# Shorter arithmetic on VectorE in a two-layer graph and mixture-of-experts network: reciprocal roots in 8 linked operations for 11, experts' ranks in 3 operations for 6

## The chip, the cores and the metric

The kernel is one program on one core of a Trainium2 chip, started once. The metric is the device time of that program in microseconds (us); a median of several executions without a profile is given, and one further execution was taken with the hardware profiler. The engines are TensorE (PE, and PEld for its weight loads), VectorE (DVE), ScalarE (ACT), GpSimd (POOL) and the queue that issues most transfers (SP). Each engine runs its own instructions in program order and waits on semaphores for the others.

## The reference

The input is a batch of 128 graphs ("tiles") of 128 nodes with 128 features, and a dense 128x128 adjacency for each. Four steps follow each other, each of the form x = x + f(...):

```python
x = x + L0_gnn(layernorm(x), adj)        # adj @ x, @ W1 (512 wide), rms norm, silu, @ W2
x = x + L0_ffn(layernorm(x), edges)      # attention over 524288 edges gives 4 scores a node; 2 of 4 experts
x = x + L1_gnn(layernorm(x), adj)        # masked softmax attention within a tile, elu
x = x + L1_ffn(layernorm(x))             # softmax over 8 gates, 2 of 8 experts
```

Every `layernorm` and the rms norm need 1/sqrt of a variance for each node. The layer norm inside the expert choice of `L0_ffn` needs it too. Both expert layers pick the two largest of 4 (or 8) values for each node, a tie going to the lower index. The experts are computed for all nodes, and the gates of those not chosen are zero.

## The kernel before

Nodes lie on the 128 partitions. Four tiles make a group (`TB = 4`), so there are 32 groups. The program has four stages one behind the other: `sort_and_gin` (tiles named front_ and sort_), which sorts the edges on VectorE while it computes the first graph layer and the first layer's expert outputs, group by group; `find_blocks` and `edge_tables` (find_, att_), which build tables; and `layers` (lay_), which does the rest. There is no planner: the order on each engine is that in which the code is written out by hand.

In `sort_and_gin`, VectorE runs for each group `sort(g, 0)`, two `hidden` (L705), `sort(g, 1)`, two `hidden`, `sort(g, 2)`, the rms root (L742, then `rsqrt`), a copy and an addition, `sort(g, 3)`, `sort(g, 4)`, then the addition of the second product (L757), which waits for TensorE, and `norms` (L716 to L723 with `rsqrt` in between). `scale` on ScalarE waits for the rms root, and the next group's TensorE work for the normalised rows.

In `layers`, each round `i` of a loop handles four blocks of edges (`attend`), the first layer's four experts of group `m = i - 2`, the attention of group `t = i - 3`, and the second layer's eight experts of group `f = i - 4`. VectorE's order in a round is:

```python
attend(b); expert(0, m, 0); elu(t); expert(0, m, 1); choose(f); expert(0, m, 2)
attend(b + 1); expert(0, m, 3); bias(0, m); end_elu(t); norms(t); expert(1, f, 0); expert(1, f, 1)
attend(b + 2); expert(1, f, 2); shift(t); expert(1, f, 3); [scores]; expert(1, f, 4)
attend(b + 3); expert(1, f, 5); weigh(m); expert(1, f, 6); expert(1, f, 7); bias(1, f); [two_best]
```

`scores` and `two_best` run in every second round only, for eight tiles at once. `choose` and `scores` call `rank`; `norms` and `scores` call `rsqrt`. `expert` is line L2174; for the second layer it waits for TensorE's product (L1800) and signals `y_added`, on which TensorE's product for the expert two further on waits. `attend` ends in the split of the messages (L1066 to L1069); TensorE's segment sum (L1777) waits for it. `shift` (L2256) waits for TensorE's gate logits (L1890).

`me.link(...)` issues an operation that raises a semaphore and lets VectorE wait for that semaphore before its next operation. `me.mark(...)` raises it without the wait, and `me.wait()` waits for all marked.

Of the kernel before, what the change touches and what calls it, by code (L numbers as in the profile page):

```python
# [9 lines left out]
I32 = mybir.dt.int32  # L10
U16 = mybir.dt.uint16
BF16 = mybir.dt.bfloat16
ALU = mybir.AluOpType
# [3 lines left out]
P = 128  # L17
LN_EPS = 1e-05
RMS_EPS = 1e-06
NEG = -9000000000000000.0  # L20
SLOPE = 0.2
TB = 4

# [66 lines left out]
def over(ap, shape):  # L90

    return ap.broadcast_to(shape)
# [8 lines left out]


def rsqrt(me, v, x, work, y):

    me.link(v.tensor_single_scalar(work.bitcast(I32), x.bitcast(I32), 1, ALU.logical_shift_right))
    me.link(v.tensor_scalar(y.bitcast(I32), work.bitcast(I32), -1.0, float(0x5F3759DF), ALU.mult, ALU.add))
    for _ in range(3):
        me.link(v.tensor_tensor(work, y, y, ALU.mult))
        me.link(v.scalar_tensor_tensor(out=work, in0=work, scalar=-0.5, in1=x, op0=ALU.mult, op1=ALU.mult))
        me.link(v.scalar_tensor_tensor(out=y, in0=work, scalar=1.5, in1=y, op0=ALU.add, op1=ALU.mult))  # L110

# [1328 lines left out]

def rank(v, me, T, E, value, mask, beat, tie, out):

    S = [P, T, E, E]
    one, other = over(value.unsqueeze(3), S), over(value.unsqueeze(2), S)
    beat = beat[:, 0:T * E * E].rearrange("p (t a b) -> p t a b", t=T, a=E)
    tie = tie[:, 0:T * E * E].rearrange("p (t a b) -> p t a b", t=T, a=E)
    lower, higher = (over(mask[:, k, 0:E, 0:E].unsqueeze(1), S) for k in range(2))
    me.mark(v.tensor_tensor(beat, other, one, ALU.is_gt))
    me.mark(v.tensor_tensor(tie, other, one, ALU.is_ge))
    me.wait()  # L1450
    me.mark(v.tensor_tensor(beat, beat, higher, ALU.mult))
    me.mark(v.tensor_tensor(tie, tie, lower, ALU.mult))
    me.wait()
    me.link(v.tensor_tensor(beat, beat, tie, ALU.add))
    me.link(v.tensor_reduce(out, beat, AX.X, ALU.add))


def layers(nc, adj, sorted_src, sorted_dst, rest_sums, first, table, made, w, keep, out):
# [10 lines left out]
    x, acc, far_parts = keep["x"], keep["acc"], keep["far"]  # L1469
# [7 lines left out]
    E0, E1 = EXP  # L1477
# [5 lines left out]
    QT = QUAD * TB  # L1483
# [4 lines left out]
    with Scope(nc, "lay") as s:  # L1488
        ident = s.sb("ident", [P, P])
        iota_b = s.sb("iota_b", [P, P], BF16)  # L1490
        node_no = s.sb("node_no", [P, tiles])
        mask = s.sb("mask", [P, 2, E1, E1])

# [31 lines left out]
        score = s.sb("score", [P, QT, E0])  # L1525
        beat = s.sb("beat", [P, max(QT * E0 * E0, TB * E1 * E1)])
        tie = s.sb("tie", [P, max(QT * E0 * E0, TB * E1 * E1)])
        ranks = s.sb("ranks", [P, QT, E0])
# [30 lines left out]
        ranks1 = s.sb("ranks1", [P, TB, E1])  # L1559
# [12 lines left out]
        consts = s.sem("consts")  # L1572
# [149 lines left out]
        def _(pool):  # L1722
# [4 lines left out]
                      allow_small_or_imprecise_dtypes=True).then_inc(consts, 1)  # L1727
            pool.memset(mask[:, :, :, :], 1.0).then_inc(consts, 1)
            pool.iota(halves[:, 0, :], [[P, tiles]], base=CLASS, channel_multiplier=1,
# [5 lines left out]
                               base=0, pattern=[[-1, P]], channel_multiplier=1).then_inc(consts, 1)  # L1735

            pool.affine_select(out=mask[:, 0, :, :], in_=mask[:, 0, :, :], compare_op=ALU.is_ge, fill=0.0,
                               base=-1, pattern=[[1, E1], [-1, E1]], channel_multiplier=0).then_inc(consts, 1)
            pool.affine_select(out=mask[:, 1, :, :], in_=mask[:, 1, :, :], compare_op=ALU.is_ge, fill=0.0,
                               base=-1, pattern=[[-1, E1], [1, E1]], channel_multiplier=0).then_inc(consts, 1)  # L1740
            for b in range(tiles):
# [6 lines left out]
                for c in range(GC):  # L1748
# [13 lines left out]
        def _(pe):  # L1762
            pe.wait_ge(consts, 9)

# [130 lines left out]
            for i in range(-1, LAST):  # L1895
                b, m, t, f = 4 * i + 2, i - QUAD, i - QUAD - 1, i - QUAD - 2
# [163 lines left out]
        def _(v):  # L2060
# [43 lines left out]
            def scores(q):  # L2104
# [39 lines left out]
                pick.link(v.tensor_reduce(small[:, :], score[:, :, :], AX.X, ALU.max))  # L2144
                rank(v, pick, QT, E0, score[:, :, :], mask, beat, tie, ranks[:, :, :])
                v.tensor_tensor(score[:, :, :], score[:, :, :], over(small[:, :].unsqueeze(2), [P, QT, E0]),
# [115 lines left out]
            def choose(g):  # L2262

                if not has(g):
                    return
                here = gates[1][:, of(g), :]
                v.wait_ge(prob_exp, g + 1)
                dense.link(v.tensor_reduce(best[:, :], here, AX.X, ALU.add))
                dense.link(v.reciprocal(best[:, :], best[:, :]))
                dense.link(v.tensor_tensor(here, here, over(best[:, :].unsqueeze(2), [P, TB, E1]), ALU.mult))  # L2270
                rank(v, dense, TB, E1, here, mask, beat, tie, ranks1[:, :, :])
                v.scalar_tensor_tensor(out=here, in0=ranks1[:, :, :], scalar=1.5, in1=here,
                                       op0=ALU.is_lt, op1=ALU.mult).then_inc(gates_ready[1], 1)

            v.wait_ge(consts, 9)
            for u in (1, 0):
# [142 lines left out]
```

## Time and profile before

| | |
|---|---|
| median of 3 executions without a profile | 3447.95 us (3446.22 to 3448.56) |
| span of the profiled execution | 3672.8 us |
| profiled span less median | 224.85 us |
| VectorE busy in the profiled span | 2761.0 us, 75% |
| TensorE busy (matmul) | 2583.2 us, 70% |
| ScalarE busy | 1723.5 us, 47% |
| mean granted TensorE clock | 0.833 of full speed |

No time other than the span is at hand for the profiled execution itself. It is 6.5% longer than the median, so its waits have to be read with care. The share of busy time is a mean over stages with different limits. The 34 us or so that VectorE spends in each group of the first stage and the 66 us or so of each round in `layers` are what the change is set against.

### The profile page before, as it was taken

To read this page: it belongs to the slowest core of one execution; us is meant where nothing else is said; L and a number is where in the kernel's file an instruction comes from. 1 tells how busy PE (TensorE), PEld (TensorE's weight loads), DVE (VectorE), ACT (ScalarE), POOL (GpSimd) and SP (SyncE) were. 2 spreads that over 40 slices of the span, in tenths; PEclk is the share of its full clock that TensorE was granted. 3 is DMA by queue.
4 is the path that set the end of the run, shared out by engine and by line. 5 is a ranking of instruction groups with operands and counts; after the bars stand their busy time and mean duration, and the time that the engine had idled before them with its cause. 6 is when DMAs were issued, how large, how long until landed. Compare 5 with 4: busy or idle time off the path is not lost.

```text
span 3672.8 us, 49655 instructions
## 1 busy us (share of the span) xinstructions
PE 2583.2 (70%) x15405; PEld 1913.6 (52%) x15406; DVE 2761.0 (75%) x8069; ACT 1723.5 (47%) x3052; POOL 1169.0 (32%) x1205
## 2 busy tenths in 40 slices
PE   1888888888888612026777777777777777777889
PEld 0666656656666401014555555555555555555666
DVE  7888778887887546367877777787787787788774
ACT  1566566665665311124454444454444544545544
POOL 0000000000000037655554545555545545555200
PEclk7899999998999855557887877878888788788899
DMA  2111111111110223223223223332232322322200
GB/s 84 34 48 47 44 46 50 44 43 38 50 38 32 72 59 77 49 62 76 63 59 78 61 63 73 66 75 65 58 78 65 73 66 62 75 64 59 76 12 9
DMA packets 228561, 210.53 MB, mean 57 GB/s; under 512 B 70781, under 2 KB 160585, under 8 KB 227657
## 3 DMA queue, kind: packets, MB, share of 16 engines
q1 hardware_dynamic: 190008, 190.83, 17.6%
q0 software_dynamic: 37280, 14.38, 4.5%
q8 instruction: 123, 2.02, 0.2%
q10 hardware_dynamic: 1008, 2.15, 0.2%
q14 instruction: 142, 1.16, 0.1%
HBM read 159.49 MB, written 47.74 MB: 56 GB/s over the span
## 4 chain that ended last, share of the span: by engine, by line
DVE 31%; PE 13%; another core or an unknown queue 8%; issue 8%; POOL 1%; ACT 1%; DVEq 0%; SPq 0%; DMA 0%; POOLq 0%; ACTq 0%
DVE keep_x L2174 7%; PE lay_b_y L1800 6%; PE lay_b_z L1791 5%; DVE lay_oh L1055 2%; POOL lay_got L1754 1%; DVE lay_oht L2079 1%; DVE lay_xn L2209 1%; DVE lay_parts L1068 1%; DVE lay_left L1067 1%; DVE lay_parts L1069 1%; DVE lay_parts L1066 1%; DVE lay_msg L1063 1%; DVE lay_stats L2198 1%; DVE lay_hp L2236 1%
## 5 line engine op out<-in xcount | busy, mean ns | idle before, releaser
L1754 POOL DMA_INDIRECT lay_got<-node_table,lay_idx x1152 | 1145.5, 994 | 928.6 <-PE lay_b_z L1791 326.3
L1800 PEld LDWEIGHTS lay_b_y<-lay_w,lay_hid 128*128 128x128 f32 x4096 | 572.1, 215 | 284.9 <-issue 271.4
L1800 PE MATMUL lay_b_y<-lay_w,lay_hid 128*128 128x128 f32 x4096 | 576.9, 298 | 114.8 <-issue 66.1
L1791 PE MATMUL lay_b_z<-lay_xin,lay_w 128*128 128x512 f32 x1024 | 599.8, 715 | 18.2 <-ACT lay_hid L1945 9.2
L1945 ACT ACTIVATE lay_hid<-lay_b_z,lay_b 128x512 f32<-128x512 f32 x512 | 332.6, 683 | 530.1 <-PE lay_b_z L1791 305.3
L2174 DVE SCALAR_TENSOR_TENSOR keep_x<-lay_b_y,lay_gates,keep_x 128x128 f32<-128x128 f32 x1024 | 287.4, 343 | 273.3 <-remote 175.4
L879 POOL MEMSET find_no_src<- 128x9 int32 x1 | 0.1, 108 | 1252.5 <-POOLq L47 1252.5
L2023 ACT ACTIVATE lay_unused<-lay_hub_wide,lay_halves 128x1152 bf16<-128x1152 uint16 x256 | 320.3, 1251 | 124.5 <-DMA lay_hub_wide<-sorted_dst 100.7
L461 PE MATMUL front_b_h<-front_xt,front_m 128*128 128x512 f32 x512 | 273.6, 666 | 58.8 <-ACT front_act_m L571 30.6
L1791 PEld LDWEIGHTS lay_b_z<-lay_xin,lay_w 128*128 128x128 f32 x1024 | 205.1, 223 | 189.3 <-issue 164.0
L217 DVE TENSOR_TENSOR sort_keys<-sort_keys 128x1024 f32<-128x1024 f32 (+2 forms) x182 | 257.4, 1414 | 37.9 <-ACT sort_keys L539 35.4
L218 DVE TENSOR_TENSOR sort_keys<-sort_keys 128x1024 f32<-128x1024 f32 (+2 forms) x182 | 256.9, 1412 | 0.0
L1777 PE MATMUL lay_b_att<-lay_parts,lay_oh 128*128 128x60 bf16 x1152 | 66.9, 210 | 236.2 <-DVE lay_parts L1069 143.5
L571 ACT ACTIVATE front_act_m<-front_b_h,front_mb 128x512 f32<-128x512 f32 x256 | 171.2, 686 | 85.4 <-PE front_b_h L461 84.9
L417 PE MATMUL front_b_h<-front_w,front_agg_t 128*128 128x512 f32 x256 | 140.4, 675 | 94.4 <-DVE front_hb L705 72.4
L480 PEld LDWEIGHTS front_b_turn<-front_m,front_act_m 128*128 128x128 f32 x1536 | 184.2, 192 | 31.6 <-issue 31.6
L461 PEld LDWEIGHTS front_b_h<-front_xt,front_m 128*128 128x128 f32 x512 | 96.2, 209 | 183.4 <-ACT front_act_m L571 98.4
L1777 PEld LDWEIGHTS lay_b_att<-lay_parts,lay_oh 128*128 128x128 bf16 x1152 | 58.9, 113 | 250.6 <-DVE lay_parts L1069 150.0
L1874 PE MATMUL lay_b_g<-lay_h,lay_att_t 128*128 128x128 f32 x256 | 63.8, 428 | 177.4 <-issue 97.5
L480 PE MATMUL front_b_turn<-front_m,front_act_m 128*128 128x128 f32 x1536 | 187.0, 275 | 0.0
L1055 DVE TENSOR_TENSOR lay_oh<-lay_iota_b,lay_low 128x1152 bf16<-128x1152 bf16 x128 | 174.7, 1365 | 0.0
L1768 PE MATMUL lay_b_att<-keep_far_parts,lay_oht 128*128 128x12 bf16 x1152 | 89.1, 204 | 107.2 <-DVE lay_oht L2079 73.0
(392 smaller groups left out, 4577.3 us busy)
## 6 DMA issues: line engine op xcount, KB each, us to landing
lay_wide<-sorted_dst SPq DMA_DIRECT2D x128, 288.0 KB
lay_hub_wide<-sorted_dst SPq DMA_DIRECT2D x128, 288.0 KB
made<-front_y SPq DMA_DIRECT2D x128, 256.0 KB, 2.0
lay_y<-made SPq DMA_DIRECT2D x32, 1024.0 KB
lay_got<-node_table,lay_idx POOLq DMA_INDIRECT x1152
front_adj<-in_adj SPq DMA_DIRECT2D x32, 256.0 KB, 3.1
keep_x<-in_x SPq DMA_DIRECT2D x32, 256.0 KB, 3.5
lay_adj<-in_adj SPq DMA_DIRECT2D x32, 256.0 KB
```

The costliest lines, as they stand in the source:

```text
L217: me.mark(v.tensor_tensor(o[:, :, 0, :], s[:, :, 0, :], s[:, :, 1, :], ALU.min))
L218: return v.tensor_tensor(o[:, :, 1, :], s[:, :, 0, :], s[:, :, 1, :], ALU.max)
L461: pe.matmul(b_h[c][:, :], m1[:, e, P * c:P * c + P], flat(xt[:, :, :]), start=True, stop=True)\
L480: mm = pe.matmul(bank[:, P * j:P * j + P], act_m[n % 2][:, c, P * j:P * j + P], m2[:, e * MK + c, :], start=(c == 0), stop=(c == MK - 1))
L571: act.activation(act_m[n % 2][:, c, :], b_h[c][:, :], ACT.Gelu, bias=mb[:, e * MK + c:e * MK + c + 1]).then_inc(act_ready, 1)
L1055: return v.tensor_tensor(out, over(iota[:, :].unsqueeze(1), S), over(lows.unsqueeze(2), S), ALU.is_equal)
L1754: pool.indirect_dma_start(out=got[:, b % RING, c, :], out_offset=None, in_=table, in_offset=bass.IndirectOffsetOnAxis(ap=idx[:, b % AHEAD, ...
L1791: pe.matmul(b_z[c][:, :], w1[:, e, P * c:P * c + P], flat(xin[g % 2][:, :, :]), start=True, stop=True).then_inc(z_done, 1)
L1800: mm = pe.matmul(b_y[n % 2][:, P * j:P * j + P], hid[n % 2][:, c, P * j:P * j + P], w2[:, e * HK + c, :], start=(c == 0), stop=(c == HK - 1))
L1945: act.activation(hid[n % 2][:, c, :], b_z[c][:, :], ACT.Gelu, bias=b1[:, e * HK + c:e * HK + c + 1]).then_inc(hid_ready, 1)
L2023: act.activation(unused[:, :], hub_wide[:, b % 2, :], ACT.Sign, bias=halves[:, u, b:b + 1], accum_out=signs[:, u, b:b + 1]).then_inc(count ...
L2174: ins = v.scalar_tensor_tensor(out=here, in0=made_here[:, P * j:P * j + P], scalar=gates[n][:, g * TB + j, e:e + 1], in1=here, op0=ALU.mul ...
```

## The change

It changes `rsqrt` and `rank`, and the constants that `rank` needs. `rsqrt` had a shift, a multiply-add on the bits as integers, and three Newton steps of three operations; it now has one multiply-add on the bits, one cubic step of four operations and one Newton step of three. `rank` compared each pair twice (greater; greater or equal), masked both results with a triangle of ones, added and reduced; it now subtracts each pair, compares the difference with 0 or the smallest normal number (`least`) by the side of the diagonal, and reduces. The buffer `tie` goes, `mask` halves and becomes `least`, and GpSimd fills it with one selection for two. Nothing is moved: the order on every engine is otherwise as before.

```diff
+LEAST = 2.0 ** -126
...
+ROOT_GUESS = float(0x5F376800)
+ROOT_1, ROOT_0, ROOT_SCALE = -3.33626263, 5.00293142, 0.375
...
 def rsqrt(me, v, x, work, y):
 
-    me.link(v.tensor_single_scalar(work.bitcast(I32), x.bitcast(I32), 1, ALU.logical_shift_right))
-    me.link(v.tensor_scalar(y.bitcast(I32), work.bitcast(I32), -1.0, float(0x5F3759DF), ALU.mult, ALU.add))
-    for _ in range(3):
-        me.link(v.tensor_tensor(work, y, y, ALU.mult))
-        me.link(v.scalar_tensor_tensor(out=work, in0=work, scalar=-0.5, in1=x, op0=ALU.mult, op1=ALU.mult))
-        me.link(v.scalar_tensor_tensor(out=y, in0=work, scalar=1.5, in1=y, op0=ALU.add, op1=ALU.mult))
+    me.link(v.tensor_scalar(y.bitcast(I32), x.bitcast(I32), -0.5, ROOT_GUESS, ALU.mult, ALU.add))
+    me.link(v.tensor_tensor(work, y, y, ALU.mult))
+    me.link(v.tensor_tensor(work, work, x, ALU.mult))
+    me.link(v.scalar_tensor_tensor(out=work, in0=work, scalar=ROOT_1, in1=work, op0=ALU.add, op1=ALU.mult))
+    me.link(v.scalar_tensor_tensor(out=y, in0=work, scalar=ROOT_0, in1=y, op0=ALU.add, op1=ALU.mult))
+    me.link(v.tensor_tensor(work, y, y, ALU.mult))
+    me.link(v.scalar_tensor_tensor(out=work, in0=work, scalar=-0.5 * ROOT_SCALE ** 3, in1=x, op0=ALU.mult, op1=ALU.mult))
+    me.link(v.scalar_tensor_tensor(out=y, in0=work, scalar=1.5 * ROOT_SCALE, in1=y, op0=ALU.add, op1=ALU.mult))
...
-def rank(v, me, T, E, value, mask, beat, tie, out):
+def rank(v, me, T, E, value, least, beat, out):
...
-    me.mark(v.tensor_tensor(beat, other, one, ALU.is_gt))
-    me.mark(v.tensor_tensor(tie, other, one, ALU.is_ge))
-    me.wait()
-    me.mark(v.tensor_tensor(beat, beat, higher, ALU.mult))
-    me.mark(v.tensor_tensor(tie, tie, lower, ALU.mult))
-    me.wait()
-    me.link(v.tensor_tensor(beat, beat, tie, ALU.add))
+    me.link(v.tensor_tensor(beat, other, one, ALU.subtract))
+    me.link(v.tensor_tensor(beat, beat, over(least[:, 0:E, 0:E].unsqueeze(1), S), ALU.is_ge))
     me.link(v.tensor_reduce(out, beat, AX.X, ALU.add))
...
-            pool.affine_select(out=mask[:, 0, :, :], in_=mask[:, 0, :, :], compare_op=ALU.is_ge, fill=0.0,
+            pool.affine_select(out=least[:, :, :], in_=least[:, :, :], compare_op=ALU.is_ge, fill=LEAST,
                                base=-1, pattern=[[1, E1], [-1, E1]], channel_multiplier=0).then_inc(consts, 1)
-            pool.affine_select(out=mask[:, 1, :, :], in_=mask[:, 1, :, :], compare_op=ALU.is_ge, fill=0.0,
-                               base=-1, pattern=[[-1, E1], [1, E1]], channel_multiplier=0).then_inc(consts, 1)
```

## Rows read from the trace of the kernel before

**Rows 1.** The page's head: span, and busy time of each engine

```profile
span 3672.8 us, 49655 instructions
PE 2583.2 (70%) x15405; PEld 1913.6 (52%) x15406; DVE 2761.0 (75%) x8069; ACT 1723.5 (47%) x3052; POOL 1169.0 (32%) x1205
```

**Rows 2.** Busy time by stretch: us; each engine (instructions); clock, DMA share, GB/s

```profile
60.00:1240.00 1180.00, 978.87 (x5767) 726.80 (x5768) 946.07 (x2026) 705.74 (x1349) 0.00 (x0) 0.93 0.12 41
1490.00:3430.00 1940.00, 1334.42 (x8012) 987.63 (x8013) 1498.06 (x5173) 862.48 (x1453) 1040.17 (x1058) 0.79 0.29 67
3430.00:3672.80 242.80, 204.96 (x1200) 153.46 (x1198) 154.48 (x559) 114.77 (x186) 2.99 (x4) 0.93 0.08 23
```

**Rows 3.** Root operations: line L105 by tile, then groups (busy, mean ns, idle before)

```profile
L105 DVE TENSOR_SCALAR front_mv<-front_mv x34: 170/174/180, 6.2 to 1228.2; 128x8 int32<-128x8 int32 x30, 128x4 int32<-128x4 int32 x4
L105 DVE TENSOR_SCALAR lay_mv<-lay_mv x33: 170/175/423, 1569.3 to 3611.6; 128x8 int32<-128x8 int32 x31, 128x4 int32<-128x4 int32 x2
L105 DVE TENSOR_SCALAR front_rin<-front_rin x32: 169/170/171, 87.8 to 1204.7; 128x4 int32<-128x4 int32 x32
L105 DVE TENSOR_SCALAR lay_small<-lay_small x16: 170/172/401, 1527.0 to 3494.4; 128x8 int32<-128x8 int32 x16
...
L109 DVE SCALAR_TENSOR_TENSOR lay_mv<-lay_mv 128x8 f32<-128x8 f32 x93 | 16.3, 176 | 4.0 <-DVE lay_mv L108 0.9
...
L108 DVE TENSOR_TENSOR front_rin<-front_rms 128x4 f32<-128x4 f32 x96 | 15.6, 162 | 3.3
...
L105 DVE TENSOR_SCALAR lay_mv<-lay_mv 128x8 int32<-128x8 int32 x31 | 7.2, 231 | 1.6 <-DVE lay_mv L2203 0.5
```

**Rows 4.** Timeline of VectorE at one call of rank in choose, and one in scores

```profile
2274.69 0.43 DVE L1448 TENSOR_TENSOR lay_beat<-lay_gates 128x256 f32<-128x256 f32 x1
...
2276.74 0.42 DVE L1455 TENSOR_REDUCE lay_ranks<-lay_beat 128x32 f32<-128x256 f32 x1
2277.20 0.24 DVE L2272 SCALAR_TENSOR_TENSOR lay_gates<-lay_ranks,lay_gates 128x32 f32<-128x32 f32 x1
...
2311.05 0.29 DVE L1448 TENSOR_TENSOR lay_beat<-lay_score 128x128 f32<-128x128 f32 x1
...
2312.43 0.29 DVE L1455 TENSOR_REDUCE lay_ranks<-lay_beat 128x32 f32<-128x128 f32 x1
2312.75 0.23 DVE L2146 TENSOR_TENSOR lay_score<-lay_score,lay_small 128x32 f32<-128x32 f32 x1
```

**Rows 5.** VectorE's waits between 66 and 1240 us; one group's timeline [idle before]

```profile
DVE keep_x L757 <- PE front_b_o L432: 61.4, 26, 5.3
...
DVE front_hb L705 <- issue: 25.7, 18, 2.8
...
523.88 0.69 DVE L757 TENSOR_TENSOR keep_x<-keep_x,front_b_o 128x512 f32<-128x512 f32 x1 [4.97 <-PE front_b_o L432]
...
535.25 1.49 DVE L705 TENSOR_TENSOR front_hb<-front_b_h,front_b 128x512 f32<-128x512 f32 x2 [1.25 <-issue]
```

**Rows 6.** Waits between 1490 and 3430 us, of VectorE, then of TensorE

```profile
DVE keep_x L2174 <- remote: 175.4, 37, 9.4
...
DVE lay_gates L2256 <- PE lay_b_g L1890: 24.5, 20, 2.5
...
PE lay_b_att L1777 <- DVE lay_parts L1069: 116.0, 24, 20.4
...
PE lay_b_y L1800 <- DVE keep_x L2174: 29.1, 13, 4.2
```

**Rows 7.** First products of two experts, TensorE's timeline; the stretches they lie in (columns as Rows 2)

```profile
2283.65 3.76 PE L1791 MATMUL lay_b_z<-lay_xin,lay_w 128*128 128x512 f32 x4
...
2296.13 1.88 PE L1791 MATMUL lay_b_z<-lay_xin,lay_w 128*128 128x512 f32 x4
...
2285.00:2290.00 5.00, 5.00 (x18) 3.47 (x17) 4.59 (x27) 1.37 (x2) 1.89 (x2) 0.54 0.17 41
...
2295.00:2300.00 5.00, 5.00 (x36) 4.04 (x35) 4.73 (x15) 1.89 (x4) 2.92 (x3) 1.00 0.44 117
```

More of the change, by code:

```diff
@@ L1445, in rank @@
     beat = beat[:, 0:T * E * E].rearrange("p (t a b) -> p t a b", t=T, a=E)
-    tie = tie[:, 0:T * E * E].rearrange("p (t a b) -> p t a b", t=T, a=E)
-    lower, higher = (over(mask[:, k, 0:E, 0:E].unsqueeze(1), S) for k in range(2))
-    me.mark(v.tensor_tensor(beat, other, one, ALU.is_gt))
-    me.mark(v.tensor_tensor(tie, other, one, ALU.is_ge))
-    me.wait()
-    me.mark(v.tensor_tensor(beat, beat, higher, ALU.mult))
-    me.mark(v.tensor_tensor(tie, tie, lower, ALU.mult))
-    me.wait()
-    me.link(v.tensor_tensor(beat, beat, tie, ALU.add))
+    me.link(v.tensor_tensor(beat, other, one, ALU.subtract))
+    me.link(v.tensor_tensor(beat, beat, over(least[:, 0:E, 0:E].unsqueeze(1), S), ALU.is_ge))
     me.link(v.tensor_reduce(out, beat, AX.X, ALU.add))
@@ L1491, in layers @@
         node_no = s.sb("node_no", [P, tiles])
-        mask = s.sb("mask", [P, 2, E1, E1])
+        least = s.sb("least", [P, E1, E1])
         base_no = s.sb("base_no", [P, tiles])
@@ L1526, in layers @@
         beat = s.sb("beat", [P, max(QT * E0 * E0, TB * E1 * E1)])
-        tie = s.sb("tie", [P, max(QT * E0 * E0, TB * E1 * E1)])
         ranks = s.sb("ranks", [P, QT, E0])
@@ L1727, in _ @@
                       allow_small_or_imprecise_dtypes=True).then_inc(consts, 1)
-            pool.memset(mask[:, :, :, :], 1.0).then_inc(consts, 1)
+            pool.memset(least[:, :, :], 0.0).then_inc(consts, 1)
             pool.iota(halves[:, 0, :], [[P, tiles]], base=CLASS, channel_multiplier=1,
@@ L1762, in _ @@
         def _(pe):
-            pe.wait_ge(consts, 9)
+            pe.wait_ge(consts, 8)
             def look_up(b):
@@ L2144, in scores @@
                 pick.link(v.tensor_reduce(small[:, :], score[:, :, :], AX.X, ALU.max))
-                rank(v, pick, QT, E0, score[:, :, :], mask, beat, tie, ranks[:, :, :])
+                rank(v, pick, QT, E0, score[:, :, :], least, beat, ranks[:, :, :])
                 v.tensor_tensor(score[:, :, :], score[:, :, :], over(small[:, :].unsqueeze(2), [P, QT, E0]),
@@ L2270, in choose @@
                 dense.link(v.tensor_tensor(here, here, over(best[:, :].unsqueeze(2), [P, TB, E1]), ALU.mult))
-                rank(v, dense, TB, E1, here, mask, beat, tie, ranks1[:, :, :])
+                rank(v, dense, TB, E1, here, least, beat, ranks1[:, :, :])
                 v.scalar_tensor_tensor(out=here, in0=ranks1[:, :, :], scalar=1.5, in1=here,
                                        op0=ALU.is_lt, op1=ALU.mult).then_inc(gates_ready[1], 1)
-            v.wait_ge(consts, 9)
+            v.wait_ge(consts, 8)
             for u in (1, 0):
```

## The prediction

> **What bounds the kernel now.** I read the page's head first: VectorE is busy 75% of the profiled span and TensorE 70%, so neither is plainly the limit [rows 1]. The table of stretches divides it. In the first stage (60 to 1240 us) TensorE is busy 979 of 1180 us and VectorE 946. In the rounds of `layers` (1490 to 3430 us) VectorE is busy 1498 of 1940 us and TensorE 1334. In the last four rounds (from 3430 us) TensorE is busy 205 of 243 us, VectorE 154 [rows 2]. So the change, which touches VectorE alone, has to be judged stage by stage, by which wait comes behind each shortened piece.
>
> In the first stage VectorE stops for TensorE about twice a group: before L757, 26 times in 32 groups for 61.4 us together, and before L705 18 times more for 25.7 us [rows 5]. The rms root stands ahead of L757 and the `norms` root ahead of L705. The group at 500 us shows both stops: 4.97 us at L757, 1.25 us at L705 [rows 5]. TensorE carries that stage.
>
> In `layers` the same view reads differently. VectorE waits for the gate logits only 24.5 us in 20 stops, and for an expert's product mostly with a releaser that the profile can't name: 175.4 us in 37 stops [rows 6]. TensorE in turn waits for VectorE's messages 116.0 us in 24 stops and for an expert's addition 29.1 us in 13 [rows 6]. The 175 us of unnamed stops, and shorter ones of their kind elsewhere, are close to the 225 us by which the profiled span exceeds the median. I take them, as a guess, for something that the profiled execution has and the others don't. Without them the stretch is some 1940 - 225 = 1715 us. VectorE's busy 1498 us fill 87% of that. Its linked operations also leave a gap behind each: 3.3 us for 96, 0.034 us each [rows 3]. For up to 5173 operations [rows 2] that is up to 176 us. So with its gaps VectorE would fill over 95% of those rounds; it carries them.
>
> **What a root costs.** There are 34 + 32 calls in the first stage and 33 + 16 in `layers` [rows 3]. Three operations of 11 go in each: the shift (L105) and two of the nine small ones. The new 8 are of kinds that the 11 had.
> - rms root: L105 0.170 us, a small one 0.162, each with a gap of 0.034 [rows 3]; 0.60 us a call, times 32 = 19.1 us.
> - `norms` in the first stage, eight columns for four: L105 0.174 [rows 3], the small ones between the 0.162 of front_rin and the 0.176 of lay_mv [rows 3], say 0.174; 0.62 us, times 34 = 21.2 us.
> - `norms` in `layers`: L105 has a mean of 0.231 there [rows 3], which the first operation of the new form might keep, for it is as much an integer operation; I count it as gone, for one of the two is. 0.231 + 0.034 + 2 x 0.206 = 0.68 us, times 33 = 22.4 us.
> - `scores`: the same L105 and the same eight columns, 0.68 us, times 16 = 10.9 us.
>
> **What a rank costs.** In `choose`, L1448 starts at 2274.69 and the line behind `rank` at 2277.20: 2.51 us. One linked operation of 256 elements takes 0.46 us from start to start (2276.74, 2277.20) [rows 4]. Three make 1.38 us, so 1.13 us are saved; times 32 groups = 36.2 us. In `scores` it is 2311.05 to 2312.75, 1.70 us, and 0.32 us for one linked operation [rows 4]; three make 0.97, so 0.73 us, times 16 = 11.7 us. The compare reads `least` repeated over the tiles, as the multiply read `mask`; no row shows it as a compare. From below it costs what the reduce costs, 0.42 us, from above nothing in rows 4 suggests more than L1448's 0.43. I take 0.42.
>
> **A rule against it.** Small operations count here by their fixed part. The row says 162 to 176 ns for 4 or 8 elements [rows 3]. The Trainium skill, page "VectorE: DVE Perf Modes", section on the TRN2 errata, has a table by which a VectorE operation takes 58 cycles and one for each element at 0.96 GHz: an estimate from it is 69 ns for 8 elements and 327 ns for 256. By that the removed work would be 115 x 0.21 + 32 x 0.98 + 16 x 0.58 = 65 us, about half, and the kernel would come out near 3410 us. The same section says that this table is too low and that fp32 tensor operations follow (N + 151)/0.96, which gives 166 and 424 ns. The trace agrees with that second line (162 to 176, and 0.42 us). My sum goes by the trace.
>
> **The rest.** GpSimd's selection less, at the start of `layers`, is a single operation; I count it at nothing. Two buffers shrink; I know of no row that gives this a price.
>
> **What reaches the end.** VectorE's work falls by 40.3 us in the first stage and by 22.4 + 10.9 + 36.2 + 11.7 = 81.2 us in `layers`, 121.5 us in all.
>
> First stage: what is saved ahead of L757 or L705 becomes a longer wait there, in 26 of 32 groups and in 18 or more at L705 [rows 5]. Where there is no stop, 6 groups of 32 for the one root and perhaps as many again for the other, 12 x 0.6 = 7 us are left, and TensorE's own work hides part. I take 6 us; the bounds are 0 and 20.
>
> `layers`: in the last four rounds TensorE has the work [rows 2] and I count nothing, which leaves 28 of 32 groups. `choose` stands right ahead of `attend(b + 1)`, whose messages TensorE waits for in most rounds [rows 6]: 28 x 1.13 = 31.7 us, all of it passed on. `norms` stands ahead of the experts 0 and 1, whose additions release TensorE's second products (13 such stops, 29.1 us [rows 6]), and ahead of nothing that VectorE waits for but the logits, which come later in that same chain: 29 x 0.68 = 19.7 us. `scores` comes behind the logits, ahead of expert 4, and is followed in the profiled execution by one of the unnamed stops; 14 of 16 calls lie where VectorE carries the round, 14 x 1.41 = 19.7 us. Together 71.1 us. Some of the last two is lost to stops that are real: I pass on 86% of them, 34 us. 31.7 + 34 = 66 us.
>
> The sum is 66 + 6 = 72 us. Against the profiled span that is 3672.8 - 72 = 3601; the span is 224.85 us above the median, which I expect to stay, and so 3447.95 - 72 = **3376 us**, 2.1% less.
>
> **The rivals.**
> - TensorE holds `layers` too (chance 0.16): the unnamed stops are true TensorE time and take in what `norms` and `scores` give. For it speaks that they stand at L2174, which waits for TensorE. Against it speaks the median. Then `choose` alone passes, and half of `norms`: 31.7 + 10 = 42, or only half of `choose` as well: 25 us. 3406 to 3423 us.
> - All of it passes, and TensorE gains besides (0.15): its gaps while it waits for messages shrink, and fewer products run at the lower clock. The same four matmul records take 3.76 us in a stretch at a granted clock of 0.54 and 1.88 us in one at 1.00 [rows 7]; one such pair in ten rounds is 19 us. With the 71.1 us of `layers` and the first stage's upper bound of 20 us that makes 71 + 20 + 19 = 110 us at most; 3338 to 3360 us.
> - No change (0.03): VectorE's time is spent at a wait everywhere, as at L757. Then also TensorE's 116 us for the messages would have to be made up elsewhere. 3441 to 3455 us.
> - Slower (0.04): the rounds shift against each other so that TensorE idles in one piece rather than in several and stays at 1.2 GHz for one more expert in each round. That expert's first product costs 3.76 - 1.88 = 1.88 us more [rows 7] and the second about as much, 3.8 us; from 72 / 3.8 = 19 rounds of 28 on it eats the gain, and in all 28 it gives 3376 + 106 = 3482 us.
> - The change doesn't do what it says: one of the new operations could be slow, a 256-element compare with a repeated operand above all. At twice 0.42 us it would cost 28 x 0.42 = 12 us, 3388 us. It is inside the range of the forecast.
>
> **Chances and range.** The forecast, 3360 to 3400 us, has 0.62; the rivals have 0.16, 0.15, 0.03 and 0.04. A range of 3350 to 3415 us holds 0.62, two thirds of the first rival and half of the second, about 0.8. A measurement of this kernel can tell about 0.2% (7 us) from no change. Faster by more than that: 0.62 + 0.16 + 0.15 = 0.93; within it 0.03; slower 0.04.
>
> **What the new profile would show.** L105 and L106 become one line, and seven lines follow it, each 0.16 to 0.18 us; VectorE has 489 instructions fewer, and is busy some 100 us less. `choose`'s three operations take 1.38 us from start to start. The first stage ends within 20 us of where it did, with longer stops before L757 and L705. The rounds of `layers` are shorter by about 1.8 us where there is no `scores` and by about 3.2 us where there is. TensorE's wait for the messages (116.0 us) falls. Were I wrong, the stops before L2174 would have grown by what `norms` and `scores` gave, or the granted clock in the rounds, 0.79 now [rows 2], would have moved.

## The result, and the profile after

| | median (range) | ratio to before, 95% interval |
|---|---|---|
| before, same chip | 3447.09 us (3446.22 to 3448.56) | |
| after | 3334.14 us (3327.39 to 3335.92) | 0.9666 [0.9652, 0.9679] |

The change makes the kernel 113 us faster. The forecast was 72 us (3376 us) with a range down to 3350: the direction is right, the size is too small by 41 us, and the time lies 16 us below the range.

The head of the page after; it answers to [rows 1].

```profile
span 3332.6 us, 49166 instructions
PE 2473.9 (74%) x15405; PEld 1845.9 (55%) x15406; DVE 2654.7 (80%) x7580; ACT 1733.2 (52%) x3052; POOL 1169.6 (35%) x1204
```

This span lies within 2 us of the median, while that of [rows 1] lay 225 us above its own. The kernel before was therefore profiled once more (the first experiment below), and this is its head:

```profile
span 3443.5 us, 49655 instructions
PE 2543.5 (74%) x15405; PEld 1888.6 (55%) x15406; DVE 2759.6 (80%) x8069; ACT 1732.8 (50%) x3052; POOL 1174.8 (34%) x1205
```

Read the two heads against each other. VectorE has 489 instructions fewer, as counted ahead, and 104.9 us less busy time; with the gap of 0.034 us behind each [rows 3] that is 105 + 17 = 122 us, and the working had 121.5. The surprise stands beside it: TensorE has the very same 15405 matmuls and is busy 69.6 us less. It executes the same work at a higher granted clock (mean 0.871 over the run, 0.85 before).

The stretches after, which answer to [rows 2] (the boundaries are moved with the program):

```profile
60.00:1240.00 1180.00, 985.23 (x5840) 732.62 (x5840) 912.80 (x1834) 711.34 (x1358) 0.00 (x0) 0.95 0.12 42
1470.00:3150.00 1680.00, 1269.58 (x8246) 953.64 (x8247) 1463.69 (x5027) 902.27 (x1502) 1049.39 (x1067) 0.85 0.34 79
```

and the rounds of before, from its second profile:

```profile
1490.00:3200.00 1710.00, 1290.56 (x7978) 959.58 (x7979) 1484.75 (x5134) 872.22 (x1453) 1048.73 (x1062) 0.82 0.34 76
```

In the rounds the granted clock goes from 0.82 to 0.85, and VectorE is still busy 87% of them, as before. The time of a round, from one start of the line that writes `hp` to the next, falls from 57.5 to 54.0 us and from 62.2 to 58.6 us: 3.5 us in both kinds, where the prediction had 1.8 us for one and 3.2 for the other. These are the commonest rounds; several after take 1 to 3 us more. The last rounds became shorter too (54.1 to 50.1, 46.5 to 43.2 and 47.1 to 45.8 us), where the prediction counted nothing. A regular group of the first stage goes from 33.2 to 32.6 us.

The waits of the rounds after, of TensorE and VectorE (engine, what waits, releaser: us in all, times, longest); they answer to [rows 6].

```profile
PE lay_b_att L1774 <- DVE lay_parts L1076: 125.3, 45, 10.9
...
PE lay_b_g L1871 <- ACT lay_att_t L1965: 122.3, 29, 5.3
...
DVE keep_x L2171 <- PE lay_b_y L1797: 77.9, 30, 2.8
...
PE lay_b_y L1797 <- DVE keep_x L2171: 44.2, 26, 3.6
...
DVE lay_gates L2253 <- PE lay_b_g L1887: 19.6, 27, 3.0
```

The same view of before, from the second profile:

```profile
PE lay_b_att L1777 <- DVE lay_parts L1069: 115.4, 46, 12.4
...
DVE keep_x L2174 <- PE lay_b_y L1800: 76.7, 36, 2.8
PE lay_b_y L1800 <- DVE keep_x L2174: 70.7, 37, 3.9
...
DVE lay_gates L2256 <- PE lay_b_g L1890: 32.1, 25, 1.9
```

No row of this view has an unnamed releaser now. VectorE's stops before L2174 are of one size before and after (76.7 and 77.9 us), so they haven't taken in what the change gave. The row that moves most is TensorE's stop ahead of an expert's second product, which waits for VectorE's addition: 70.7 to 44.2 us. VectorE's stop for the gate logits goes from 32.1 to 19.6 us; the fifth experiment will show what that row is worth. The prediction said that TensorE's wait for the messages would fall. It rose by 10 us; that TensorE arrives there earlier is likely and not shown.

### The profile page after: what moved, and what is told of

Same layout as the page of the kernel before. It is cut to its first block, busy times and chain, and to the rows that moved or that the text cites. A ratio compares the mean times of both kernels' runs of the same rounds, so it can differ in the third digit from the quotient of the medians.

```text
span 3332.6 us, 49166 instructions
## 1 busy us (share of the span) xinstructions
PE 2473.9 (74%) x15405; PEld 1845.9 (55%) x15406; DVE 2654.7 (80%) x7580; ACT 1733.2 (52%) x3052; POOL 1169.6 (35%) x1204
## 3 DMA queue, kind: packets, MB, share of 16 engines
q1 hardware_dynamic: 190008, 190.83, 19.1%
q8 instruction: 123, 2.02, 0.2%
## 4 chain that ended last, share of the span: by engine, by line
DVE 29%; PE 19%; issue 6%; POOL 5%; ACT 1%; DVEq 0%; DMA 0%; POOLq 0%; ACTq 0%
PE lay_b_y L1797 9%; DVE keep_x L2171 7%; PE lay_b_z L1788 7%; POOL lay_got L1751 5%; DVE lay_xn L2206 2%; DVE lay_stats L2195 1%; DVE lay_oh L1062 1%; DVE lay_oht L2076 1%; DVE lay_left L1074 1%; DVE lay_parts L1075 1%; DVE lay_parts L1073 1%; PE lay_b_att L1765 1%; PE lay_b_g L1887 1%; DVE lay_parts L1076 1%; DVE lay_msg L1070 1%
## 5 line engine op out<-in xcount | busy, mean ns | idle before, releaser
L1797 PEld LDWEIGHTS lay_b_y<-lay_w,lay_hid 128*128 128x128 f32 x4096 | 529.4, 203 | 209.8 <-issue 170.5
L1797 PE MATMUL lay_b_y<-lay_w,lay_hid 128*128 128x128 f32 x4096 | 533.2, 286 | 55.8 <-DVE keep_x L2171 51.5
L1788 PE MATMUL lay_b_z<-lay_xin,lay_w 128*128 128x512 f32 x1024 | 560.7, 675 | 1.2 <-ACT lay_hid L1942 1.2
L2020 ACT ACTIVATE lay_unused<-lay_hub_wide,lay_halves 128x1152 bf16<-128x1152 uint16 x256 | 320.0, 1250 | 109.2 <-DMA lay_hub_wide<-sorted_dst 104.9
L1788 PEld LDWEIGHTS lay_b_z<-lay_xin,lay_w 128*128 128x128 f32 x1024 | 196.3, 213 | 155.7 <-issue 144.9
L433 PE MATMUL front_b_ht<-front_diag,front_hb 128*128 128x128 f32 x1024 | 131.7, 282 | 34.0 <-ACT front_diag L569 21.6
```

The lines of the kernel that those rows point to most:

```text
L1788: pe.matmul(b_z[c][:, :], w1[:, e, P * c:P * c + P], flat(xin[g % 2][:, :, :]), start=True, stop=True).then_inc(z_done, 1)
L1797: mm = pe.matmul(b_y[n % 2][:, P * j:P * j + P], hid[n % 2][:, c, P * j:P * j + P], w2[:, e * HK + c, :], start=(c == 0), stop=(c == HK - 1))
L2020: act.activation(unused[:, :], hub_wide[:, b % 2, :], ACT.Sign, bias=halves[:, u, b:b + 1], accum_out=signs[:, u, b:b + 1]).then_inc(count ...
```

## The experiments

Two questions are open: which calls gave more than their work, and through what. My theory: `norms` stands directly ahead of an addition for which TensorE stops, and a shorter stop also spares a product at 1.2 GHz, so that this work counts twice. The rivals: the two smaller buffers moved others in memory; or VectorE's work passes fully everywhere and the working lost time in its bounds alone. The parts are edits of the kernel before, with the new root and rank beside the old ones as `rsqrt_new` and `rank_new`, or of the changed kernel where it says so; the diffs leave out the definitions and, for the rank, the buffer `least` and its filling by GpSimd; "before" is always that of the same chip.

**Nothing changed, profiled again.**

> The kernel before, unchanged, to get a second profile of it. Theory A (the profiled execution of before was 225 us longer for a reason of that execution): the span falls to about 3445 us, the stops before the experts' additions with a releaser that can't be named (175.4 us) go to under 20 us, and the time is that of before within 0.2%. Rival (those stops are in every execution of before, and the change removed them): the span stays near 3670 us and the stops stay.

Measured: 3445.22 us (before 3449.27), ratio 0.9995 [0.9985, 1.0005]; span 3443.5 us. The guess on the profiled execution holds: the extra 225 us and the unnamed stops belonged to that execution.

**Roots alone, everywhere.** All four calls take the new root, the ranks stay old.

```diff
+                rsqrt_new(gin, v, mv[:, lo:hi, 2], mv[:, lo:hi, 3], rstd[:, lo:hi])
...
+                rsqrt_new(gin, v, rin[:, 0, :], rin[:, 1, :], rms[:, :])
...
+                rsqrt_new(pick, v, small[:, :], small2[:, :], rs[:, :])
...
+                rsqrt_new(dense, v, mv[:, lo:hi, 2], mv[:, lo:hi, 3], rstd[:, lo:hi])
```

> Only the roots by the new form, in all four places; ranks as before. VectorE's work falls by 19 + 21 + 22 + 11 = 73 us by my sum. Theory A (VectorE carries the rounds, TensorE the first stage): of the 33 us in the rounds nearly all passes, of the 40 us in the first stage some 14 us: 3447 - 47 = 3400 us. Theory B (a multiplier: each us taken off VectorE in the rounds also shortens TensorE's idle time and lifts its clock, 1.2 us for 1): 3394 us. Theory C (only what stands right ahead of the messages passes): 3430 us or more, for no root stands there.

Measured: 3376.16 us (before 3449.27), 0.9794 [0.9777, 0.9810]: 73 us from 73.6 us of removed work.

**Ranks alone, everywhere.** The changed kernel with the old root put back.

```diff
-    me.link(v.tensor_scalar(y.bitcast(I32), x.bitcast(I32), -0.5, ROOT_GUESS, ALU.mult, ALU.add))
+    me.link(v.tensor_single_scalar(work.bitcast(I32), x.bitcast(I32), 1, ALU.logical_shift_right))
...
```

> Only the ranks by the new form, in both places; roots as before. By my sum 36 + 12 = 48 us less on VectorE. Theory A: 3447 - 46 = 3401 us. Theory B: 3447 - 58 = 3389 us. Theory C: 3415 us, the ranks in choose alone. If roots and ranks alone add up to 113 us the parts are independent; if they add up to less, each alone leaves a stop that both together clear.

Measured: 3395.32 us (before 3449.27), 0.9852 [0.9827, 0.9876]: 54 us from 47.9 us of work. The two halves add up to 127 us against the whole's 113; by the ratios it is 122 against 115, and the three intervals allow for that difference. The roots aren't simply passed on, though; the next four runs show how unequal their parts are.

**Roots of the first stage alone.**

```diff
-                rsqrt(gin, v, mv[:, lo:hi, 2], mv[:, lo:hi, 3], rstd[:, lo:hi])
+                rsqrt_new(gin, v, mv[:, lo:hi, 2], mv[:, lo:hi, 3], rstd[:, lo:hi])
...
-                rsqrt(gin, v, rin[:, 0, :], rin[:, 1, :], rms[:, :])
+                rsqrt_new(gin, v, rin[:, 0, :], rin[:, 1, :], rms[:, :])
```

> The new root only in the first stage (rms root and norms there), nothing changed in the rounds. By my sum 40 us of VectorE's work. My prediction passed on 6 us of it: 3441 us. The two profiles at hand say that the next stage began 14 us earlier: 3433 us. If TensorE did not carry that stage at all it would be 3407 us.

Measured: 3429.59 us (before 3449.27), 0.9949 [0.9933, 0.9966]: 17.6 us by the ratio and 19.7 by the medians, from 40.3 us of work. The prediction had 6.

**Root of `norms` in the rounds alone.**

```diff
-                rsqrt(dense, v, mv[:, lo:hi, 2], mv[:, lo:hi, 3], rstd[:, lo:hi])
+                rsqrt_new(dense, v, mv[:, lo:hi, 2], mv[:, lo:hi, 3], rstd[:, lo:hi])
```

> The new root only in norms within the rounds: 22 us of VectorE's work by my sum. The roots of all places gave 71 us and those of the first stage 18, so that norms and scores within the rounds gave some 53 us for 33. Theory A (one for one) wants 3447 - 22 = 3425 us. Theory B (norms stands ahead of the additions that release TensorE and of the rows that it turns next; an earlier release also saves TensorE time at its lower clock) wants 35 to 42 us: 3405 to 3412 us.

Measured: 3401.8 us (before 3448.45), 0.9867 [0.9851, 0.9884]: 46 us, from 22 us of work. Two to one. Here the main part of the missed time shows. The two matmul groups of the experts, of before (second profile) and of this kernel (busy, mean ns of one | idle time ahead of them, and what ended it):

```profile
L1791 PE MATMUL lay_b_z<-lay_xin,lay_w 128*128 128x512 f32 x1024 | 593.4, 709 | 3.9 <-ACT lay_hid L1945 3.9
...
L1800 PE MATMUL lay_b_y<-lay_w,lay_hid 128*128 128x128 f32 x4096 | 553.1, 293 | 99.3 <-DVE keep_x L2174 91.7 <-ACT lay_hid L1945 7.6
```

```profile
L1807 PE MATMUL lay_b_z<-lay_xin,lay_w 128*128 128x512 f32 x1024 | 589.1, 705 | 1.2 <-ACT lay_hid L1961 1.2
...
L1816 PE MATMUL lay_b_y<-lay_w,lay_hid 128*128 128x128 f32 x4096 | 539.7, 289 | 73.5 <-DVE keep_x L2190 68.0 <-ACT lay_hid L1961 5.5
```

The stops ahead of the second products fall by 25.8 us. That is about what VectorE no longer does there (33 x 0.62 to 0.68 = 20 to 22 us). Besides, the products themselves take 13.4 + 4.3 = 17.7 us less, for the same matmuls. One such place in each kernel's timeline of TensorE (start, us, what, [stop ahead of it]), before first:

```profile
2226.78 1.88 PE L1791 MATMUL lay_b_z<-lay_xin,lay_w 128*128 128x512 f32 x4
2231.56 3.38 PE L1800 MATMUL lay_b_y<-lay_w,lay_hid 128*128 128x128 f32 x16 [2.90 <-DVE keep_x L2174]
```

```profile
2334.47 2.02 PE L1816 MATMUL lay_b_y<-lay_w,lay_hid 128*128 128x128 f32 x16 [1.92 <-DVE keep_x L2190]
```

and the four microseconds around each (columns as [rows 2]), before first:

```profile
2231.00:2235.00 4.00, 3.44 (x18) 3.47 (x19) 3.63 (x14) 0.34 (x1) 1.89 (x2) 0.57 0.63 152
```

```profile
2334.00:2338.00 4.00, 3.53 (x23) 2.90 (x24) 3.63 (x15) 2.00 (x5) 2.94 (x4) 1.00 0.63 147
```

Both kernels go through the same products. Behind a stop of 2.90 us the sixteen matmuls take 3.38 us at a granted clock of 0.57, so mostly at 1.2 GHz; behind one of 1.92 us they take 2.02 us at 1.00, that is at 2.4 GHz. Counted over both timelines, 19 of 42 products with a stop for VectorE take more than 2.3 us before, and 6 of 43 here. The slow ones among them are all products of expert 2: of its 32, 22 take more than 2.3 us before and 8 here, with a stop or without.

VectorE's own stops show what the second half of the 46 us is. These are its stops for the gate logits over the whole run, before first:

```profile
DVE lay_gates L2256 <- PE lay_b_g L1890: 49.7, 30, 4.7
```

```profile
DVE lay_gates L2272 <- PE lay_b_g L1906: 27.7, 29, 4.4
```

VectorE has some 22 us less to do and stops 22.0 us less for the logits; its stops for the experts' products are the same (133.2 and 133.7 us). That makes 44 of the 46 us. TensorE issues the logits behind the products of experts 2 and 3, so a slow product of expert 2 makes them late. Taken round by round over the trace of before, VectorE stops 2.19 us for them on average in the 22 rounds with a slow product of expert 2, and 0.16 us in the 9 others.

**Rank of `choose` alone.**

```diff
-                rank(v, dense, TB, E1, here, mask, beat, tie, ranks1[:, :, :])
+                rank_new(v, dense, TB, E1, here, least, beat, ranks1[:, :, :])
```

> The new rank only in choose: 36 us of VectorE's work by my sum, right ahead of the messages that TensorE waits for. Both theories want it passed in full: 3447 - 36 = 3411 us by theory A, up to 3395 us by theory B. If much less, the stop of TensorE for the messages is not what sets the rounds.

Measured: 3410.15 us (before 3448.45), 0.9897 [0.9878, 0.9916]: 36 to 38 us, from 36.2 us of work. One to one, as forecast for the rounds, and in the last ones too: from the fourth last start of the line that writes `hp` to the end it is 210.6 us for 216.1.

**Root and rank of `scores` alone.**

```diff
-                rsqrt(pick, v, small[:, :], small2[:, :], rs[:, :])
+                rsqrt_new(pick, v, small[:, :], small2[:, :], rs[:, :])
...
-                rank(v, pick, QT, E0, score[:, :, :], mask, beat, tie, ranks[:, :, :])
+                rank_new(v, pick, QT, E0, score[:, :, :], least, beat, ranks[:, :, :])
```

> Only scores changed, root and rank both, in 16 rounds: 23 us by my sum. Theory A 3424 us. Theory B: behind the logits and ahead of expert 4, where TensorE doesn't wait for it, so less than in full; 3430 us. If this is where the extra comes from: under 3415 us.

Measured: 3438.24 us (before 3448.45), 0.9971 [0.9961, 0.9981]: 10 us, from 22.6 us of work. VectorE's stops for the gate logits grow from 49.7 us to

```profile
DVE lay_gates L2287 <- PE lay_b_g L1921: 66.0, 31, 4.8
```

and take in 16 of the 22.6 us; its stops for the experts' products fall by 6 (133.2 to 127.1 us). The clock is in this too: expert 2's product takes more than 2.3 us in 30 of 32 groups, for 22 before, and expert 1's in none, for 21 before. So the slow product moved from expert 1 to expert 2, nearer ahead of the logits. Why it moved isn't shown.

**The layout.** The changed kernel with two buffers that nothing uses, as large as what the change took away.

```diff
+        spare = s.sb("spare", [P, E1, E1])
+        tie = s.sb("tie", [P, max(QT * E0 * E0, TB * E1 * E1)])
```

> The changed kernel with the two buffers kept at their old size (unused), so that every later buffer lies where it did before. All theories but one: 3334 us, as the changed kernel. If the place of the buffers gave part of the gain (113 us measured for 121 of VectorE's work, of which the first stage passes only a part), it is slower than 3341 us.

Measured: 3332.8 us (before 3448.45), 0.9668 [0.9652, 0.9684], the same as the change itself. That rival is out.

**Root of the rms norm alone (first stage).**

```diff
-                rsqrt(gin, v, rin[:, 0, :], rin[:, 1, :], rms[:, :])
+                rsqrt_new(gin, v, rin[:, 0, :], rin[:, 1, :], rms[:, :])
```

> The new root only at the rms norm of the first stage, 19 us of VectorE's work by my sum. Both roots of that stage gave 18 us of 40, and 16 of its groups went from 33.2 to 32.6 us, the price of one root. Theory P: it is the rms root that passes (ScalarE's diagonal waits for it, TensorE for the diagonal, and L757 for TensorE), the norms root only lengthens the stop at L705: 3447 - 16 = 3431 us. Rival Q, the reasoning of my prediction (both end in stops, what passes comes from groups without one): half of the 18 us, 3438 us.

Measured: 3434.36 us (before 3448.13), 0.9962 [0.9948, 0.9976]: 13 to 14 us of 19.1; some 4 to 6 us are left for the other root's 21.2. A chain explains the first. ScalarE builds a diagonal from the rms values, and TensorE's L426 waits for it. Waits between 60 and 1240 us of before (second profile):

```profile
PE front_b_ht L426 <- ACT front_diag L562: 29.0, 32, 5.4
...
DVE front_hb L705 <- issue: 25.7, 18, 2.7
```

of this kernel:

```profile
DVE front_hb L721 <- issue: 25.6, 18, 2.7
...
PE front_b_ht L442 <- ACT front_diag L578: 21.6, 32, 4.8
```

and of the changed kernel, with both roots:

```profile
DVE front_hb L712 <- issue: 39.7, 20, 3.4
...
PE front_b_ht L433 <- ACT front_diag L569: 21.6, 32, 4.8
```

The rms root shortens TensorE's own stop (29.0 to 21.6 us) and so brings the product forward that releases L757. VectorE's stop at L757 still grows in this stretch, from 62.3 to 66.8 us; of 19.1 us less work that leaves 14.6, about what the kernel gained. With the other root as well VectorE's stop at its second wait is 14.1 us longer (25.6 to 39.7 us), two thirds of that root's 21.2, as forecast. The other root was not run alone.

**No change on VectorE, but TensorE kept at work.** If the clock is what a stop costs besides its length, then before must gain when only the stop is filled. 24 bf16 matmuls, 128x128x128, whose results nobody reads, are issued for expert 2 right ahead of the wait for the addition, into bank `b_g`; the added wait makes sure that VectorE has read it.

```diff
+                if e == 2 and has(g + 1):
+                    pe.wait_ge(hm_ready, g + 2)
+                    for k in range(24):
+                        pe.matmul(b_g[:, 0:P], iota_b[:, :], iota_b[:, :], start=True, stop=True)
```

> The kernel before, with 24 small bf16 products (results unused) put into TensorE's idle time ahead of the second expert product that waits for VectorE's additions behind norms; VectorE's work is that of before. Theory B (part of what the shorter norms gave is that the product behind this stop runs at the full clock): the product behind the stop takes 1.95 us, not 3.4, in most rounds, and the kernel gains 10 to 35 us: 3412 to 3437 us. Theory A (only VectorE's time counts): 3447 us or a little more.

Measured: 3412.66 us (before 3448.13), 0.9903 [0.9886, 0.9921]: 35 us less with 744 matmuls more and VectorE's instructions untouched. The timeline at such a place:

```profile
2275.01 1.88 PE L1791 MATMUL lay_b_z<-lay_xin,lay_w 128*128 128x512 f32 x4
2276.73 1.50 PE L1796 MATMUL lay_b_g<-lay_iota_b 128*128 128x128 bf16 x24
2279.49 2.05 PE L1807 MATMUL lay_b_y<-lay_w,lay_hid 128*128 128x128 f32 x16 [1.26 <-DVE keep_x L2181]
```

The product takes 2.05 us again, and only 3 of 43 are slow. The groups:

```profile
L1791 PE MATMUL lay_b_z<-lay_xin,lay_w 128*128 128x512 f32 x1024 | 581.6, 697 | 4.0 <-ACT lay_hid L1952 4.0
...
L1807 PE MATMUL lay_b_y<-lay_w,lay_hid 128*128 128x128 f32 x4096 | 528.1, 285 | 56.2 <-DVE keep_x L2181 56.2
```

Against before the products take 25.0 + 11.8 = 37 us less. And VectorE's stops for the gate logits, 49.7 us before, are

```profile
DVE lay_gates L2263 <- PE lay_b_g L1897: 16.7, 5, 4.2
```

That is 33.0 us less, nearly all of the 35: the clock of one product reaches the end through this stop. The Trainium skill, page "TensorE: Matmul & The Clock Gate", section "Why this matters for your kernels", warns of idle gaps between bursts of matmuls, after which the lower clock comes back. The rows agree: 22 slow products of 32 with the stop empty, 3 with part of it filled.

**Three operations put back, ahead of the product.** The changed kernel with three linked eight-column multiplies, whose result nobody reads, behind each root of `norms`.

```diff
                 rsqrt(dense, v, mv[:, lo:hi, 2], mv[:, lo:hi, 3], rstd[:, lo:hi])
+                for _ in range(3):
+                    dense.link(v.tensor_tensor(mv[:, lo:hi, 3], mv[:, lo:hi, 2], mv[:, lo:hi, 2], ALU.mult))
```

> The changed kernel, with three linked eight-column operations (results unused) put back in norms of the rounds, ahead of the normalised rows; 0.62 us a round, 20 us in all. Theory B: it loses what the new root in norms gave, some 45 us: 3379 us. Theory A: 20 us, 3354 us.

Measured: 3375.48 us (before 3448.13), 0.9784 [0.9766, 0.9802]: 41 us above the changed kernel's 3334.14, for 33 x 0.62 = 20 us of work.

**The same three, behind the additions of experts 0 and 1.**

```diff
                 expert(1, f, 0)
                 expert(1, f, 1)
+                if has(t) or has(t + 1):
+                    lo, hi = 0 if has(t) else TB, 2 * TB if has(t + 1) else TB
+                    for _ in range(3):
+                        dense.link(v.tensor_tensor(mv[:, lo:hi, 3], mv[:, lo:hi, 2], mv[:, lo:hi, 2], ALU.mult))
```

> The same three operations, but behind the additions of experts 0 and 1, where no TensorE product waits at once. Theory B (the place makes the price): 0 to 15 us more than the changed kernel, 3334 to 3349 us, and clearly less than with the operations ahead. Theory A: 3354 us in both places.

Measured: 3357.16 us (before 3448.13), 0.9733 [0.9716, 0.9749]: 23 us above the changed kernel, where the theory had 0 to 15. The same instructions cost 18 us less when they stand a few lines later. The second products, ahead first, then behind, then in the changed kernel:

```profile
L1797 PE MATMUL lay_b_y<-lay_w,lay_hid 128*128 128x128 f32 x4096 | 558.4, 295 | 81.2 <-DVE keep_x L2171 77.8 <-ACT lay_hid L1942 3.5
```

```profile
L1797 PE MATMUL lay_b_y<-lay_w,lay_hid 128*128 128x128 f32 x4096 | 554.6, 294 | 69.3 <-DVE keep_x L2171 65.0 <-ACT lay_hid L1942 4.3
```

```profile
L1797 PE MATMUL lay_b_y<-lay_w,lay_hid 128*128 128x128 f32 x4096 | 533.2, 286 | 55.8 <-DVE keep_x L2171 51.5 <-ACT lay_hid L1942 4.3
```

Of the 18 us between the two, 11.9 are TensorE's stops and 3.8 product time. But the products are slow in both (16 of 30 with a stop ahead, 18 of 37 behind, 7 of 30 in the changed kernel). VectorE's stops for the gate logits, in the same order:

```profile
DVE lay_gates L2255 <- PE lay_b_g L1887: 49.5, 31, 4.6
```

```profile
DVE lay_gates L2253 <- PE lay_b_g L1887: 40.4, 21, 4.5
```

```profile
DVE lay_gates L2253 <- PE lay_b_g L1887: 35.0, 31, 4.4
```

With the 20 us of work they give 35 of the 41 us and 26 for the 23. So the place decides what an operation on VectorE costs; the clock isn't all of the difference between these two.

**The fillers in the changed kernel.** The edit with the 24 matmuls for expert 2, made to the changed kernel.

> The changed kernel with the same 24 filler products at the same place. In the kernel before they gave 35 us, in the changed kernel fewer products behind that stop run slowly (6 for 14 in the profiles). If the extra of norms (47 us for 22 of work) and the gain by the fillers are the same time, the fillers give much less here: under 15 us, 3320 to 3334 us. If they are different things, 35 us again: 3299 us.

Measured: 3325.3 us (before 3445.83), 0.9653 [0.9637, 0.9670]. The interval overlaps that of the change, 0.9666 [0.9652, 0.9679]. What gave before 35 us gives here 4 to 9 at most. The changed kernel had less to win there: 9 slow products of expert 2, of which one is left here, where before had 22. (The profiled execution is the fastest of the four, 3315.72 us, so its rows show more than the median gained: second products 526.9 us for 533.2, first ones 547.4 for 560.7.) The clock gain of the shorter root and that of the fillers are largely one and the same.

**Fillers in a second stop as well.** 44 more matmuls ahead of the products that wait for the attention (L1871).

```diff
+                if has(t):
+                    after(pe, bias_added[0], min(m, groups))
+                    after(pe, bias_added[1], min(f, groups))
+                    for k in range(44):
+                        pe.matmul(b_b[:, 0:P], iota_b[:, :], iota_b[:, :], start=True, stop=True)
                 apply_att(t)
```

> The changed kernel with fillers at that stop and 44 more in the stop of some 5 us ahead of the attention's product, once a round. If TensorE's lower clock behind that long stop sets part of the round, 20 to 60 us less than the changed kernel: 3275 to 3314 us. If VectorE alone carries that part of the round (choose and the messages), nothing more than with the first fillers.

Measured: 3329.21 us (before 3445.83), 0.9668 [0.9650, 0.9686]: no more. TensorE's groups at L1871, with one filler and with two:

```profile
L1878 PE MATMUL lay_b_g<-lay_h,lay_att_t 128*128 128x128 f32 x256 | 63.1, 426 | 123.5 <-ACT lay_att_t L1972 123.5
```

```profile
L1878 PE MATMUL lay_b_g<-lay_h,lay_att_t 128*128 128x128 f32 x256 | 36.2, 284 | 15.9 <-ACT lay_att_t L1976 15.9
```

Those products run at the higher clock now (284 ns each for 426), most of the stop is gone from the row, the mean clock rose from 0.873 to 0.892, and the time is the same. VectorE stops only 3.1 us in all for what these products compute (L2240 of the run with one filler), so it has nothing to gain there, and TensorE's own time turns into a longer wait for VectorE's messages, 218.4 us for 167.6.

## Why the prediction was wrong

- **VectorE's removed work, 121.5 us:** right; 104.9 us of busy time and 489 gaps. The pieces too: `choose`'s three operations and the gap behind them run from 2223.67 to 2225.04, 1.37 us (forecast 1.38), and the compare costs what the difference costs.

```profile
2223.67 0.42 DVE L1453 TENSOR_TENSOR lay_beat<-lay_gates 128x256 f32<-128x256 f32 x1
2224.12 0.42 DVE L1454 TENSOR_TENSOR lay_beat<-lay_beat,lay_least 128x256 f32<-128x256 f32 x1
2224.58 0.42 DVE L1455 TENSOR_REDUCE lay_ranks<-lay_beat 128x32 f32<-128x256 f32 x1
2225.04 0.19 DVE L2269 SCALAR_TENSOR_TENSOR lay_gates<-lay_ranks,lay_gates 128x32 f32<-128x32 f32 x1
```

- **The extra of the profiled span belongs to that execution:** a guess that held (3443.5 us the second time).
- **The step that failed: "29 x 0.68 = 19.7 us" for `norms`, passed on at 86%, 17 us.** Alone, this root gave 46 us (fifth experiment). That accounts for 29 of the 41 us that were missed. The work was sized rightly; the step took a microsecond of VectorE to be worth at most one of the kernel. But TensorE stops for the addition behind `norms`, and what VectorE spares there shortens the stop and keeps the product of expert 2 that follows it at 2.4 GHz; the logits come behind that product, and VectorE's stop for them fell by 22.0 us, as much again as the work. The prediction named the logits as the one thing behind `norms` that VectorE waits for, and used this stop only as a place where a saving is lost. Balance of TensorE over the two spans, 44.2 us apart: 21.1 us less busy, 25.8 less at this stop, 13.8 more at the messages (183.0 for 169.2), 11.1 less in the other stops. That the clock matters is shown by the fillers (35 us without any change on VectorE, 33.0 of them at the same stop), that the place matters by the operations put back (41 and 23 us for the same 20). How the 22.0 us divide between the earlier start of expert 2's product and its higher clock isn't settled: products are 17.7 us shorter in this run.
- **The rival "TensorE gains besides" was the right mechanism at the wrong place and size.** It looked at the wait for the messages, which grew, and priced ten products at the lower clock, 19 us in all, with 3338 us as its end. The granted clock moved from 0.82 to 0.85, which the prediction had named as a sign against itself, and TensorE's busy time fell by 70 us.
- **First stage, "I take 6 us": mis-sized, measured 18 to 20.** It is near the upper bound of 20. The step "what is saved ahead of L757 or L705 becomes a longer wait there" fails for most of the rms root (4.5 us more at L757, of 19.1): L757's releaser is itself behind that root, through ScalarE's diagonal and L426. It holds for two thirds of the other root (14.1 of 21.2 us at L705).
- **`choose`, 31.7 us passed on in full: right;** measured 36 to 38. The 4 to 6 us more are the last four rounds, on which it counted nothing: 5.5 us with `choose` alone. There TensorE waits for VectorE too: of the 91.7 us of its stops for the additions before, 70.7 lie in the stretch of the rounds above and 21.0 behind it.
- **`scores`, 17 us after the 86%: too large; measured 10.** VectorE's stops for the logits, a round later, grew by 16 us when `scores` alone was changed (49.7 to 66.0 us) and so took most of it in, with slow products of expert 2 in 30 groups for 22. It looks like the mechanism of `norms` the other way round; no run took it apart. The argument on "the unnamed stops" behind `scores` was about that one execution.
- Sum of the parts as measured alone: 46 + 37 + 10 + 19 = 112 us, and 113 together. That they meet so closely is partly luck: the two halves gave 127, and `norms` and `scores` move the same stop in opposite directions (with the whole change it is 35.0 us, 14.7 less than before). The prediction's error is likewise a net one: 29 us too low for `norms`, 13 for the first stage and 5 for `choose`, 7 too high for `scores`.

## What to carry to other kernels

An operation on VectorE has no one price. Ahead of the addition for which TensorE had stopped it cost two for one here, behind it about one for one, and some 5 for 21 where VectorE itself stopped soon after (the first stage's other root, by difference). A stop of the other engine alone doesn't make the price double. `scores` also stands ahead of an addition for which TensorE stopped (expert 6, 14 times, 17.9 us), but no product behind that stop was slow, and `scores` gave less than half of its work. So ask of each place who waits for what comes next, whether that engine comes out of the wait at the lower clock, and whether the first engine waits for its work later in the round. Before a stop is called one that takes in the saving, follow its releaser back: if the releaser hangs on the very operation that gets shorter, the saving passes through. A profile whose span is several per cent above the median of the runs should be taken again before its waits are read.

## What the runs showed of the hardware

- A short stop of TensorE inside a busy stretch can bring it back to 1.2 GHz: sixteen matmuls took 3.38 us behind a stop of 2.90 us, with a granted clock of 0.57 around them, and 2.02 us behind one of 1.92 us, with 1.00. Filling part of the stop with 24 matmuls, 1.5 us, that compute nothing of use was worth 35 us of 3448.
- A higher mean clock is no gain by itself. With fillers in two stops it rose from 0.873 to 0.892 and the time stayed; with `scores` alone changed, fewer products of all experts were slow (43 for 58 of 256), but more of those ahead of the logits (30 for 22).
- The first operation of the new root, an integer operation of eight columns, has two durations at two places of the changed kernel (lowest/median/highest ns):

```profile
L110 DVE TENSOR_SCALAR lay_rs<-lay_small x16: 171/356/366, 1474.6 to 3161.8; 128x8 int32<-128x8 int32 x16
L110 DVE TENSOR_SCALAR lay_rstd<-lay_mv x33: 170/172/173, 1510.3 to 3273.3; 128x8 int32<-128x8 int32 x31, 128x4 int32<-128x4 int32 x2
```

In `scores` it takes twice as long in more than half of its calls. It isn't the operation or the place alone: in the run with `scores` alone changed all 16 calls take 170 to 172 ns. The cause wasn't tried. In the kernel before, single calls of the old form's first operation were as slow (up to 401 ns at L105 in [rows 3]), but their median was 172.
